# The causal mask of the second score pass, moved from PE products to a GpSimd select on the exponentials

## The reference, cut to what matters

```python
qh = (q @ Wq.T + bq).reshape(Bb, Lq, H, hd).transpose(0, 2, 1, 3)
kh = (kv @ Wk.T + bk).reshape(Bb, Lkv, H, hd).transpose(0, 2, 1, 3)
vh = (kv @ Wv.T + bv).reshape(Bb, Lkv, H, hd).transpose(0, 2, 1, 3)
scores = jnp.einsum('bhqd,bhkd->bhqk', qh, kh) * scale
mask = jnp.arange(Lkv)[None, :] <= jnp.arange(Lq)[:, None]
scores = jnp.where(mask[None, None], scores, -jnp.inf)
attn = jax.nn.softmax(scores, axis=-1)
out = jnp.einsum('bhqk,bhkd->bhqd', attn, vh)
...
return out @ Wo.T + bo
...
x = x + jnp.tanh(g_xattn[0]) * attention(ctx, layernorm(x), ...)
x = x + jnp.tanh(g_ffn[0]) * ffn(layernorm(x), ...)
```

## Time and profile before

| what | value |
|---|---|
| median of 3 runs | 836.72 us (832.86 to 837.49) |
| profiled execution / its span | 827.2 us / 825.5 us |
| PE, DVE, ACT, POOL busy | 624.0, 321.9, 221.0, 203.4 us |
| chain that ended last, by engine | PE 64%, DVE 11%, DMA 11%, POOL 7% |
| pass 0 (exp and max) | about 119 to 162 us |
| pass 1, pass 2 | about 213 to 257 us, 307 to 348 us |
| last pass (exp alone) | about 371 to 402 us |

### The profile page before, as it was taken

How to read it: one execution, slowest core, us unless ns; L and a number is a source line. 1 busy time by engine, 2 the same in 40 slices (tenths; PEclk the granted TensorE clock), 3 DMA queues, 4 the chain that set the end, 5 groups by cost and what they waited for, 6 DMA issues and landing times.

```text
span 825.5 us, 10012 instructions
## 1 busy us (share of the span) xinstructions
PE 624.0 (76%) x3136; PEld 382.6 (46%) x3136; DVE 321.9 (39%) x848; ACT 221.0 (27%) x475; POOL 203.4 (25%) x227
## 2 busy tenths in 40 slices
PE   1646869973699449949721799999999999197758
PEld 1323335543354335544421466666666666055536
DVE  1462866734475417740269122222222222033213
ACT  1101016610364006507400222222222222032212
POOL 6237000060001600000000533333333331644240
PEclk9978559996699959979955555555555555589869
DMA  6179930029400790023072333333333332332121
GB/s 199 37 129 164 129 54 2 2 89 115 79 1 3 138 118 2 1 80 102 0 139 43 96 99 99 102 99 100 102 103 99 101 102 73 95 89 78 49 77 39
DMA packets 55392, 66.63 MB, mean 81 GB/s; under 512 B 6365, under 2 KB 49226, under 8 KB 55338
## 3 DMA queue, kind: packets, MB, share of 16 engines
q1 hardware_dynamic: 48060, 47.15, 28.5%
q0 software_dynamic: 7280, 18.84, 8.9%
HBM read 42.99 MB, written 22.68 MB: 80 GB/s over the span
## 4 chain that ended last, share of the span: by engine, by line
PE 64%; DVE 11%; DMA 11%; POOL 7%; issue 3%; SPq 2%; ACT 1%; POOLq 0%; DVEq 0%; ACTq 0%
PE ps_max L798 12%; PE ps_a L808 7%; PE ps_d L808 6%; PE ps_max L648 5%; PE ps_exp L668 5%; DMA QK<-parts_dram 5%; PE ps_exp L788 5%; PE ps_pv L686 5%; PE ps_max L833 3%; DMA xs_dram<-XN 2%; POOL VA L465 2%; PE ps_max L652 2%; DVE MX L944 2%; PE ps_exp L673 2%; PE ps_d L594 2%
## 5 line engine op out<-in xcount | busy, mean ns | idle before, releaser
L451 POOL DMA_INDIRECT PT<-xs_dram,CX x93 | 87.7, 943 | 319.1 <-DVE CX L1111 172.8
L944 DVE TENSOR_REDUCE MX<-ps_max 128x1 f32<-128x384 f32 (+3 forms) x176 | 108.4, 641 | 58.3 <-PE ps_max L652 56.7
L531 ACT ACTIVATE PT<-ps_exp 128x512 f32<-128x512 f32 (+1 forms) x176 | 94.8, 561 | 93.1 <-PE ps_exp L673 88.3
L798 PE MATMUL ps_max<-PT 128*64 128x128 f32 x372 | 103.9, 435 | 0.3 <-issue 0.3
L648 PE MATMUL ps_max<-QK 96*128 96x128 bf16 (+3 forms) x256 | 76.4, 356 | 29.4 <-DMA QK<-parts_dram 25.2
L798 PEld LDWEIGHTS ps_max<-PT 128*64 128x64 f32 x372 | 66.7, 219 | 31.3 <-issue 31.3
L553 ACT ACTIVATE PT<-ps_exp 128x256 f32<-128x256 f32 x93 | 35.7, 384 | 139.1 <-PE ps_exp L788 139.1
L668 PE MATMUL ps_exp<-QK 99*128 99x512 bf16 (+3 forms) x256 | 67.7, 323 | 4.2 <-DMA QK<-MT 4.2
L426 POOL TENSOR_TENSOR R<-Q,PARTS 128x512 f32<-128x512 f32 x16 | 18.5, 1154 | 206.6 <-ACT PARTS L488 205.7
L788 PE MATMUL ps_exp<-ident,PT 128*128 128x128 f32 x186 | 59.2, 422 | 5.4 <-DMA PT<-xs_dram,CX 5.4
L788 PEld LDWEIGHTS ps_exp<-ident,PT 128*128 128x128 f32 x186 | 42.5, 230 | 31.9 <-issue 22.8
(11 more groups left out here) (187 smaller groups left out, 863.4 us busy)
## 6 DMA issues: line engine op xcount, KB each, us to landing
QK<-parts_dram SPq DMA_DIRECT2D x48, 256.0 KB, 14.1
ys_dram<-PT SPq DMA_DIRECT2D x93, 128.0 KB, 1.7
parts_dram<-PARTS SPq DMA_DIRECT2D x16, 384.0 KB, 2.7
X<-in_x_dram SPq DMA_DIRECT2D x4, 512.0 KB, 11.3
CX<-in_ctx_dram SPq DMA_DIRECT2D x4, 512.0 KB, 5.0
xs_dram<-XN SPq DMA_DIRECT2D x4, 512.0 KB, 10.7
out_dram<-X SPq DMA_DIRECT2D x16, 128.0 KB, 1.7
PT<-xs_dram,CX POOLq DMA_INDIRECT x93, 3.1
```

Of the source, the lines that this page charges most:

```text
L451: nc.gpsimd.indirect_dma_start(out=GX[:, i % 4, :], out_offset=None, in_=xs_dram[:, :], in_offset=bass.IndirectOffsetOnAxis(ap=IDX[:, i:i ...
L531: nc.scalar.activation(PT[:, grp % 2, heads[0]:heads[-1] + 1, START[j]:START[j] + w], ps_exp[:, k % EXP_BANKS, 0:w * len(heads)].rearrange ...
L798: last = nc.tensor.matmul(ps_max[0:HID, r % 2, 0:P], W1S[:, r % 2, HID * a:HID * (a + 1)], GXT[:, r % 2, a, :], start=(a == 0), stop=(a == 1))
L944: nc.vector.tensor_reduce(MX[:, b % 2, hg, i, heads[0]:heads[-1] + 1], ps_max[:, k % MAX_BANKS, 0:w * len(heads)].rearrange("p (h s) -> p ...
```

## The change

The 16 mask products of every group (256 in all) go. POOL instead sets the exponentials above the diagonal to zero, in `PT`, by one `affine_select` for each group and key tile: the diagonal blocks of four heads, 4 x 128 columns of f32 on 128 partitions, in place; 64 selects in all. Each waits for `exp_free` of the last exp unit of its j, then for its own completion (`cut_done`); PV waits for `cut_done` in place of `exp_free`. The selects of batch b stand on POOL after the bias addition of b and ahead of `split(b + 2)`. The constant `maskt` and its two instructions go.

```diff
+        cut_done = sem("cut_done")
...
-            link(nc.gpsimd.memset(maskt[:, :], 0.0))
-            const(nc.gpsimd.affine_select(out=maskt[:, :], in_=maskt[:, :], compare_op=ALU.is_ge, fill=MASKED,
-                                          base=0, pattern=[[1, P]], channel_multiplier=-1))
...
+                for hg in range(NG):
+                    for j in range(TB):
+
+                        last = max(u for u, (jj, _) in enumerate(EXP_UNITS) if jj == j)
+                        pool.wait_ge(exp_free, NU * (NG * b + hg) + last + 1)
+                        blk = PT[:, (NG * b + hg) % 2, :, START[j]:START[j] + P]
+                        nc.gpsimd.affine_select(out=blk, in_=blk, compare_op=ALU.is_ge, fill=0.0, base=0,
+                                                pattern=[[0, HG], [1, P]], channel_multiplier=-1).then_inc(cut_done, 1)
+                        pool.wait_ge(cut_done, TB * (NG * b + hg) + j + 1)
                 if b + 2 < B:
                     split(b + 2)
...
                 for a, h in enumerate(heads):
-                    nc.tensor.matmul(ps_exp[:, k % EXP_BANKS, w * a:w * (a + 1)],
-                                     k_of(b, HG * hg + h, ROWS_MAX, P * j, P * (j + 1)),
-                                     q_of(b, HG * hg + h, ROWS_MAX, P * j, S), start=(a == 0), stop=False,
-                                     skip_group_check=True)
-                for a, h in enumerate(heads):
-                    last = nc.tensor.matmul(ps_exp[:, k % EXP_BANKS, w * a:w * a + P], identb[:, :], maskt[:, :],
-                                            start=False, stop=(a == len(heads) - 1), skip_group_check=True)
+                    last = nc.tensor.matmul(ps_exp[:, k % EXP_BANKS, w * a:w * (a + 1)],
+                                            k_of(b, HG * hg + h, ROWS_MAX, P * j, P * (j + 1)),
+                                            q_of(b, HG * hg + h, ROWS_MAX, P * j, S), start=True, stop=True)
...
-                last = max(u for u, (jj, _) in enumerate(EXP_UNITS) if jj == j)
-                pe.wait_ge(exp_free, NU * grp + last + 1)
+                pe.wait_ge(cut_done, TB * grp + j + 1)
```

More of the change, by code:

```diff
@@ L88, in build @@
         maskb = sb("maskb", [P, P], BF16)
-        maskt = sb("maskt", [P, P], BF16)
         trib = sb("trib", [P, P], BF16)
@@ L661, in exp_unit @@
                     pe.wait_ge(mt_in[b % 2], 48 * (b // 2 + 1))
-                    pe.wait_ge(consts, 4)
+                    pe.wait_ge(consts, 3)
                     pe.wait_ge(ones_in, 32)
```

## The result

In the same comparison the kernel before took 835.12 us (median of 6 runs, 832.86 to 837.49) and the changed one 839.27 us (838.2 to 839.97): ratio 1.005, 95% interval 1.0031 to 1.007, some 4 us slower. The forecast was 831 with a range of 825 to 838. In three later comparisons the changed kernel came out at 1.0018 (1.0005 to 1.0031), 1.0054 (1.0034 to 1.0075) and 1.0024 (1.0001 to 1.0048): slower each time, by 1.5 to 4.5 us.

The account below looks back on a forecast made before the run. The chain of waits was read as lying on PE for most of the span. 6.1 + 0.2 - 0.5 = 5.8 us off the profiled 827.2 gave 821.4; from the median of 836.72 the forecast was 831, range 825 to 838.

Parts of the forecast that it names:

- The mask products and the walked group: Groups with max units, passes 0 to 2: without masks each steady group gains 0.47 us, together 6.1 us.
- masks hidden anyway: Rival: DVE and ACT bind more than walked, so only 1 to 3 us remain, 835; chance 0.10.
- PE alone binds: Rival: waits at m9 and m5 shrink too, so 11 to 13 us are gained, 825; chance 0.08.
- The select: On POOL: each 512-column select takes 0.61 us, at most 1.15, with a handover of 0.06 each way.
- PV waiting for POOL in passes 0 to 2: Sign of being wrong: PV held up by the selects in passes with max units, where they were forecast as hidden.
- The rival with 1.15 us: Rival: selects take 1.15 us, delaying PV in the last pass and pass ends by about 5 us, 836; chance 0.20.
- even 1.15 fits: Groups with max units: a select of 1.15 us would still be done before PV 3 wants it.
- Queued on POOL behind the selects: On POOL after each batch's selects: the next bias addition and split(b + 2) follow, and no split is delayed.
- The last pass: Exp units alone, selects bare: 0.23 us gained a group, 0.7 in three, 0.45 lost at the end, net +0.2 us.
- The term for the start: Start of the last pass: without masks PE waits for ACT, so full clock comes later, mean cost 0.5 us.
- Full clock not granted in the last pass: Rival: pauses keep the last pass at the lower clock, 12 to 15 us more, 843; chance 0.12.

Follow-up runs that it names:

- E7: E6 with every select done twice, one after the other, in passes 0 to 2: 826.29 us, ratio 0.9985 to the kernel before.
- E5: The changed kernel again, no edit, with a second profile: 829.03 us, ratio 1.0018 to the kernel before.
- E1: The changed kernel with the bias addition of batch 3 early, ahead of the selects of pass 2: 822.51 us, ratio 0.995 to the kernel before.
- E13: The changed kernel with ten spare PE products while PE waits for the split maxima of batch 3: 836.94 us, ratio 1.0012 to the kernel before.
- E9: E1 again, in one comparison with the changed kernel: 834.61 us, ratio 0.9984 to the kernel before.
- E10: The changed kernel again, no edit, in one comparison with E9: 839.37 us, ratio 1.0054 to the kernel before.
- E15: E6 again, in another comparison: 833.16 us, ratio 0.9955 to the kernel before.
- E2: The kernel before, with only the bias addition of batch 3 held until the last exponential of pass 2: 830.38 us, ratio 1.0039.
- E4: The kernel before, masks kept, with the selects added on GpSimd and PV waiting for them: 834.83 us, ratio 1.0085.
- E12: The changed kernel with batch 3's bias added early and a one-input GpSimd product at the late place: 835.98 us, ratio 1.0005 to the kernel before.
- E8: The kernel before, with selects in place of PE masks in the last pass only: 828.49 us, ratio 1.0013.
- E3: The changed kernel without selects, so nothing above the diagonal is cut, and bias additions at their old place: 820.68 us, ratio 0.9924 to the kernel before.
- E6: The changed kernel with PE masks kept in the last pass and the bias addition of batch 3 early: 821.43 us, ratio 0.9927 to the kernel before.
- E11: The changed kernel with the bias addition of batch 3 held until DVE finished pass 2's split maxima: 833.49 us, ratio 0.999 to the kernel before.

## Why the prediction was wrong

By its own steps:

- *The mask products and the walked group.* Right. -0.47 us a group was forecast, -0.48 measured; u7 to PV 1 -0.17 and -0.19; m9 0.75 behind the reduction and 0.74. For passes 0 to 2 the forecast was 6.1 us. From MP 0 to the last copy of pass 2, four profiles with masks and no selects there take 231.7 to 233.7 us (mean 232.9), twelve without masks, with single selects or none, 226.1 to 228.7 (mean 227.3): 5.6 us. The rival "masks hidden anyway" falls, and so does "PE alone binds".
- *The select.* Right: 0.61 forecast from the earlier trace rows, 0.636 measured, 64 times, 40.7 us. The handovers are 0.13 from ACT and 0.05 to PE, for 0.06 each. PV's weight loads wait for it 15 times, 6.4 us in all, at most 0.82. My sign of being wrong, "PV waiting for POOL in passes 0 to 2", came in small: 0.25 and 0.35 us at each pass's end, nothing inside the groups. In the last pass PV 2 waits too, not PV 1 alone. The rival with 1.15 us falls, although E7 shows that my "even 1.15 fits" held inside the groups alone.
- *Queued on POOL behind the selects.* **This is the step that failed.** It said that behind the selects stand the bias addition and `split(b + 2)`, that the split is not delayed, and "both cost and gain nothing". The split was argued; the addition was not. The addition of batch 3 moved by 60 us, from a place where the DVE step beside it kept its 0.75 us to the one where PE waits for a chain of short DVE steps. I had even written that at a pass's end "PE goes on with DVE's split maxima", and looked only at PV beside it, and only at pass 0, where `split(2)` still waits for its input when the selects end. My account of GpSimd, idle from 119 to 402 us, was read from two windows; it did the splits and additions of later batches from 170 to 282 us, outside the windows that I had looked at.
- *Its price.* 2.0 us directly (2.77 for 0.70 or 0.75). Then the clock: 2.5 us to the first copy of pass 3 (E5 against E1), which E13 shows to hang on PE's pause. By medians E1 took away 4.8 us in one comparison (E9, E10) and 6.5 across two. Another 2.4 us lie behind pass 3 in E5 against E1, and these are not shown to be the collision's: E9 and E15 have no collision and lose 2.6 and 1.3 us there, E2, E4 and E12 have one and lose nothing against E1. Their cause stays open.
- *The last pass.* Sign right in the groups, sizes off. A group gains 0.15, not 0.23, as PV 1 starts 1.68 us behind u7 and not 1.60; the end loses 0.75 from u7 to the copy, not 0.45. The term for the start, 0.5, was the larger miss: the first copy of pass 3 comes 1.0 to 1.8 us later (E1, E9, E8), and 0.5 is lost behind the pass. Its reason, that missing masks hold back the full clock, is not borne out: E3 has no masks and starts as before (33.0 us), E6 and E15 keep the masks in the last pass and still start 0.9 to 1.0 us late (33.8 and 33.7). What makes the start late is open; at least part comes with the selects. In all I had 0.3 us of loss where the profiles show 2.6 to 2.8 (E8, E1).
- *Full clock not granted in the last pass.* The slower rival did not come: 1.00 from 376.19 until 403.49, past the end of the pass. The clock was lost in the short dependent work between the passes instead, where no rival of mine had put it.

The Trainium skill states the rule that I should have weighed, in "SBUF — State Buffer" (Who interferes with whom): a cast or a scalar operation of VectorE in its two-port mode, or one with two inputs in SBUF, shares a port pair with GpSimd, and whichever is issued first keeps it for its whole instruction. By that rule the cast of 0.19 us waits for the addition's end; the traces agree in the changed kernel (2.22 us, ending 0.05 us behind the addition), in E2 (2.05 for the first scalar operation, ending 0.03 us behind the addition), and in E11, where DVE reads from PSUM and isn't held. They do not agree fully in E12: the cast came through after 0.91 us of a GpSimd operation that the profile shows for 2.79, and a subtraction with two inputs in SBUF was not held at all.

Had I priced the addition at 2 us and left the clock out, the sum would have been about 833. With the clock up to the first copy of pass 3 and the last pass as measured it is 5.6 - 4.5 - 2.6 = -1.5, a loss of 1.5 us, and 3.9 with the 2.4 us behind pass 3. The four comparisons gave losses of 1.5 to 4.5 us. With before at 828 (E5) the changed kernel took 829.03 us, inside the forecast's range, with the same step wrong: there the number would have been right by luck.

## What to carry to other kernels

Work that is inserted in an engine's stream delays all that stands behind it: list every instruction there by name, find in the trace where each runs now, and ask what it will run beside. An engine that looks free is not free where its work can hold up another: two tenths of a microsecond on a critical handover (the cast, 0.19) became nearly the whole length of the other's instruction (2.22 of 2.37). Where PE's clock hangs on it, a pause of 2 us costs more than 2 us; and before two profiles are subtracted, check a stretch that the change can't touch.

Here the change is worth having with two corrections: the bias additions at their old place, and the masks left on PE in the pass that has no max units beside (E6 and E15: 0.9927 and 0.9955). What the second correction adds to the first is not shown by the times: the first alone had 0.995 and 0.9984 (E1 and E9).

## What the runs showed of the hardware that I had not expected

- A GpSimd addition of 128x1024 f32 with two SBUF inputs (2.37 us) holds a DVE cast of 0.19 us for 2.22, or four scalar operations of 0.40 for 2.28 (the first of them for 2.05). A one-input operation of 2.79 us held the cast for 0.91. A select of 0.64 us stretches the same four from 0.40 to 0.52. DVE operations with an input in PSUM run beside the addition unchanged (0.26 and 0.42 us).
- The same eight products took 1.97 us or 3.75 us, depending on whether PE had waited 0.8 or 2.8 us before that stretch, and 3.57 after a wait of 1.5 (E12); ten spare products in the wait brought back the first.
- DVE started one copy of the last stage after 4.2 to 6.4 us of idle time in the comparisons with before at 835 us, and after 1.0 to 1.2 in those at 828, on the same kernels and once on the same chip; the profile names no instruction that releases it. What decides between the two levels stays open, as does the lower clock behind pass 3.
